# An attention and mixture-of-experts layer on one core: who issues the expert weights' loads, and where in the program

## The reference

```python
x = hidden_states                                   # 2 x 2048 x 512, float32
x = x + layernorm(attention(layernorm(x)))          # linear attention, 16 heads, 4 kv heads, D = 128
x = x + layernorm(moe(layernorm(x), wg, w1, v1, w2))

def moe(x):                                         # 4096 tokens, 32 experts, top 8, H = 512, F = 192
    scores = softmax(x @ wg.T)
    weights, idx = top_k(scores, 8); weights /= sum(weights)
    for each expert e, over the rows sent to it:
        h = silu(rows @ w1[e]) * (rows @ v1[e])
        out[token] += (h @ w2[e]) * weight
```

## Time and profile before

| | us |
|---|---|
| median of 3 runs | 2455.93 (2454.94 to 2457.64) |
| the profiled execution | 2444.98 |
| its span, first to last instruction | 2443.3 |
| TensorE busy in the span | 2227.0 (91%) |
| VectorE, ScalarE, GpSimd busy | 1486.4, 1233.1, 956.2 |

### The profile page before, as it was taken

One profiled execution on the slowest core, in us unless ns is written; L12 is line 12 of the kernel. 1 busy time (PEld: TensorE's weight loads), 2 busy tenths in 40 slices (PEclk: granted clock), 3 DMA queues, 4 the chain that ended last, 5 costly groups with the idle time before them and its releaser, 6 DMA issues.

```text
span 2443.3 us, 64606 instructions
## 1 busy us (share of the span) xinstructions
PE 2227.0 (91%) x11850; PEld 1919.5 (79%) x11851; DVE 1486.4 (61%) x4836; ACT 1233.1 (50%) x2643; POOL 956.2 (39%) x1128
## 2 busy tenths in 40 slices
PE   7999899999999999995699999989999899988980
PEld 5888588888868888884598888878889788978970
DVE  4455567777777777775555555565555655555546
ACT  3344456665656666663344454455444544444433
POOL 1222015555535555556233334333344333433432
PEclk9999899999999999997899999999999999999995
DMA  3233202333343233233898888877777877776767
GB/s 122 78 120 120 78 27 104 117 119 117 119 149 127 106 117 131 101 135 138 255 225 193 180 203 184 182 196 175 144 157 145 191 160 166 141 168 137 142 106 296
DMA packets 165230, 358.64 MB, mean 147 GB/s; under 512 B 21168, under 2 KB 21168, under 8 KB 165040
## 3 DMA queue, kind: packets, MB, share of 16 engines
q0 software_dynamic: 60512, 144.74, 28.5%
q1 hardware_dynamic: 91216, 173.89, 23.7%
q10 hardware_dynamic: 13440, 39.33, 4.9%
HBM read 178.21 MB, written 179.66 MB: 146 GB/s over the span
## 4 chain that ended last, share of the span: by engine, by line
PE 32%; DMA 7%; issue 6%; ACTq 2%; DVE 2%; POOL 2%; DVEq 1%; ACT 1%; POOLq 1%; SPq 0%
DMA moe_sum<-Y,aidx 6%; PE bank L469 6%; PE bank L471 5%; PE bank L470 5%; PE bank L460 4%; PE bank L486 2%; PE bank L479 2%; PE bank L490 2%; PE bank L488 2%; PE bank L487 2%; PE bank L489 2%; DMA LATE<-w_in 1%; POOL sorted_rows L1543 1%; ACTq L329 1%; ACT BIG L596 1%
## 5 line engine op out<-in xcount | busy, mean ns | idle before, releaser
L1477 POOL DMA_INDIRECT moe_sum<-Y,aidx x276 | 432.2, 1566 | 776.0 <-DMA moe_sum<-Y,aidx 416.7
L933 PE MATMUL bank<-WB,XH 128*128 128x512 f32 x1536 | 477.1, 392 | 0.0
L469 PE MATMUL bank<-WB,XL 128*128 x1104 | 398.2, 361 | 0.0
L471 PE MATMUL bank<-WB,XH 128*128 x1104 | 373.4, 338 | 0.0
L470 PE MATMUL bank<-WB,XH 128*128 x1104 | 371.5, 337 | 0.0
L933 PEld LDWEIGHTS bank<-WB,XH 128*128 128x128 f32 x1536 | 290.4, 189 | 58.3 <-issue 0.7
L933 PE MATMUL bank<-WB,XL 128*128 128x512 f32 x768 | 316.1, 412 | 10.3 <-DVE XL L1259 10.3
L933 PE MATMUL bank<-WB,SH 128*128 128x512 f32 x1024 | 318.1, 392 | 0.0
L713 DVE SCALAR_TENSOR_TENSOR BIG<-BIG,bank x276 | 95.9, 348 | 351.8 <-ACT BIG L531 274.1
L1543 POOL DMA_INDIRECT sorted_rows<-BIG,pos x256 | 265.6, 1038 | 94.6 <-issue 94.6
L531 ACT ACTIVATE BIG<-bank x276 | 91.3, 331 | 341.7 <-PE bank L471 319.9
(11 more groups left out here) (218 smaller groups left out, 4260.3 us busy)
## 6 DMA issues: line engine op xcount, KB each, us to landing
BIG<-sorted_rows SPq DMA_DIRECT2D x278, 274.0 KB
Y<-x_in SPq DMA_DIRECT2D x64, 256.0 KB, 2.8
RAW<-w_in ACTq DMA_DIRECT2D x15, 768.0 KB
LATE<-w_in ACTq DMA_DIRECT2D x15, 768.0 KB
sorted_rows<-BIG SPq DMA_DIRECT2D x33, 274.0 KB
moe_sum<-LATE SPq DMA_DIRECT2D x34, 256.0 KB, 3.0
LATE<-x_in SPq DMA_DIRECT2D x32, 256.0 KB
RAW<-wo_in SPq DMA_DIRECT2D x16, 512.0 KB, 3.7
```

The source lines that it names most:

```text
L469: nc.tensor.matmul(eu[s][:, 0:UP], XL[:, s, k, :], wh, start=k == 0, stop=False)
L471: last = nc.tensor.matmul(eu[s][:, 0:UP], XH[:, s, k, :], wl, start=False, stop=k == KC - 1)
L933: last = nc.tensor.matmul(ps, w, m, start=start and i == 0, stop=stop and i == len(terms) - 1)
L1477: nc.gpsimd.indirect_dma_start(acc_dram[:, :], bass.IndirectOffsetOnAxis(aidx[:, s:s + 1], 0), rows, None, compute_op=ALU.add).then_inc(s_ ...
```

## The change

SyncE's loop no longer goes by groups of four tiles but by expert. For expert e it waits for a fill of pads, issues the fill of expert e+8, waits on `s_elo` and issues the four loads of the weights of expert e+3; for 14 of the experts it then issues a load of `after_attention`; then it issues the row loads of tiles first+6 to first+n+5. Eight fills and the first six row loads stand ahead of the loop. The row ring keeps its four slots and the waits on `s_T` and `s_wr`. The four semaphores of the row loads become one, `s_ld`; SyncE waits before tiles g and g+1 (g even) until all loads before g have landed, and TensorE waits for the loads by pairs. ScalarE keeps the conversions and loses the wait on `s_elo` and the loads between the pieces. Six more entries of `at_tile` are set to zero, and four more row loads are issued at the end.

```diff
--- before.py
+++ after.py
@@ -38,6 +38,7 @@
 PIECES = [(k * UP, UP) for k in range(KC)] + [(W13, HID), (W13 + HID, HID)]
 FRING = 8
 XRING = 14
+AHEAD = 6
 FOUT = 4
 YSLOTS, RSLOTS = 4, 4
 
@@ -156,7 +157,7 @@
         rank = sb("rank", [P, EXPERTS])
         posf = sb("posf", [P, TOP_K])
         pos = sb("pos", [P, 2, TOP_K], u32)
-        AT, ES = MAX_TILES + 2, 4 * EXPERTS
+        AT, ES = MAX_TILES + 2 + AHEAD, 4 * EXPERTS
         tn = bq[:, 0:ES].rearrange("p (i n) -> p i n", i=4)
         step = bq[:, ES:ES + 2 * EXPERTS].rearrange("p (i n) -> p i n", i=2)
         table = bq[0:1, 2 * ES:2 * ES + 4 * EXPERTS].bitcast(i32).rearrange("p (i n) -> p i n", i=4)
@@ -242,11 +243,11 @@
 
         s_ewr, s_ehi, s_elo = [sem("ew_loaded0"), sem("ew_loaded1")], sem("ew_high"), sem("ew_low")
         s_pad0 = sem("padding_ready")
-        s_fill, s_fillx = [sem("pads_filled0"), sem("pads_filled1")], sem("spare_page_filled")
-        s_ld = [sem(f"rows_loaded{i}") for i in range(RSLOTS)]
+        s_fill, s_fill0, s_fillx = [sem("pads_filled0"), sem("pads_filled1")], sem("first_pads_filled"), sem("spare_page_filled")
+        s_ld = sem("rows_loaded")
         s_wr, s_T, s_exh, s_exl = sem("row_tails"), sem("e_transposed"), sem("e_high"), sem("e_low")
         s_U, s_sg, s_h = sem("e_up"), sem("e_silu"), sem("e_act")
         s_H, s_hh, s_hl = sem("e_act_transposed"), sem("e_act_high"), sem("e_act_low")
@@ -296,13 +297,16 @@
             return not isinstance(t, int) or 0 <= t - lag < TILES
 
 
+        def expert_word(eng, e):
+            word = eng.value_load(table[0:1, 0, bass.ds(e, 1)], min_val=512 + 32768, max_val=512 * 32768 - 1)
+            return word & 511, (word >> 9) & 63, word >> 15
         def each_expert(eng, convert, body):
 
             eng.wait_ge(s_tabd, 1)
 
             def one(e, q):
-                word = eng.value_load(table[0:1, 0, bass.ds(e, 1)], min_val=512 + 32768, max_val=512 * 32768 - 1)
-                first, n, before = word & 511, (word >> 9) & 63, word >> 15
+                first, n, before = expert_word(eng, e)
                 convert(e, q, before)
                 body(e, q, first, n)
                 return first + n
@@ -352,17 +356,19 @@
                 last.then_inc(s_elo, 1)
 
         def moe_sp(sp):
-            def fill_pads(e, i):
+            def fill_pads(e, done):
                 row = sp.value_load(table[0:1, 2, bass.ds(e, 1)], min_val=0, max_val=PAGES * PAGE)
-                sp.dma_start(sorted_dram[bass.ds(row, P), :], padrow[:, 0, :]).then_inc(s_fill[i], 16)
-            def load_rows(g, i):
+                sp.dma_start(sorted_dram[bass.ds(row, P), :], padrow[:, 0, :]).then_inc(done, 16)
+            def load_rows(g):
                 row = sp.value_load(at_tile[0:1, 2, bass.ds(g + 2, 1)], min_val=0, max_val=PAGES * PAGE)
                 sp.wait_ge(s_T, g + 1)
                 stand(sp)
                 sp.wait_ge(s_wr, g + 1)
                 stand(sp)
-                sp.dma_start(xr[:, i, :], sorted_dram[bass.ds(row, P), :]).then_inc(s_ld[i], 16)
+                wait(sp, s_ld, g // 2 * 32 if isinstance(g, int) else (g >> 1) * 32)
+                stand(sp)
+                sp.dma_start(BIG[:, at(XR, g & (RSLOTS - 1), ROW, ROW)], sorted_dram[bass.ds(row, P), :]).then_inc(s_ld, 16)
 
             def load_x2(f, r):
                 sp.dma_start(fx[:, bass.ds(r, 1), :, :].rearrange("p a j n -> p (a j) n"),
@@ -379,35 +385,51 @@
             sp.wait_ge(s_pad0, 5)
             sp.dma_start(sorted_dram[EXTRA * PAGE:EXTRA * PAGE + P, :], padrow[:, 1, :]).then_inc(s_fillx, 16)
             sp.wait_ge(s_tabd, 1)
-            for e in range(2):
-                fill_pads(e, e)
+            for e in range(AHEAD + 2):
+                fill_pads(e, s_fill0)
             for i in range(2):
                 sp.wait_ge(s_sc[i], TILES // 2 * TOP_K * 16)
             sp.wait_ge(s_fillx, 16)
+            sp.wait_ge(s_fill0, 16 * (AHEAD + 2))
             sp.wait_ge(s_tiles, 1)
-            def quad(p, fill=False):
-                for i in range(RSLOTS):
-                    g = RSLOTS * p + i
-                    if fill:
-                        sp.wait_ge(s_fill[i % 2], 32 * p + 16 * (i // 2) + 16)
-                        stand(sp)
-                    load_rows(g, i)
-                    if fill and (not isinstance(g, int) or g + 2 < EXPERTS):
-                        fill_pads(g + 2, i % 2)
-            FILLS = EXPERTS // RSLOTS
-            with sp.Fori(0, FILLS - 1) as p:
-                quad(p, True)
-            quad(FILLS - 1, True)
-            with sp.Fori(0, XRING) as f:
-                quad(f + FILLS)
-                load_x2(f, f)
-            quads = sp.value_load(pair_n[0:1, 0:1], min_val=TOKENS * TOP_K // P // 2, max_val=PAGES // 2) >> 1
-            with sp.Fori(FILLS + XRING, quads) as p:
-                quad(p)
+            for g in range(AHEAD):
+                load_rows(g)
             for i in range(2):
-                load_rows(RSLOTS * quads + i, i)
+                sp.sem_inc(s_fill[i], 16)
+            def body(e, q, first, n, x2=None):
+                i = q % 2
+                if not isinstance(e, int) or e + AHEAD < EXPERTS:
+                    sp.wait_ge(s_fill[i], (e - i) * 8 + 16)
+                    stand(sp)
+                if not isinstance(e, int) or e + AHEAD + 2 < EXPERTS:
+                    fill_pads(e + AHEAD + 2, s_fill[i])
+                if not isinstance(e, int) or e + 3 < EXPERTS:
+                    sp.wait_ge(s_elo, e + 2)
+                    stand(sp)
+                    load_weights(sp, e + 3, (q + 1) % 2)
+                if x2 is not None:
+                    load_x2(x2, x2)
+                with sp.Fori(0, n) as k:
+                    load_rows(nc.s_assert_within(first + k + AHEAD, AHEAD, MAX_TILES + AHEAD - 1))
+            with sp.Fori(0, 3) as r:
+                for q in range(WSETS):
+                    e = r * WSETS + q
+                    first, n, _ = expert_word(sp, e)
+                    body(e, q, first, n, e)
+            with sp.Fori(3, 6) as r:
+                for q in range(WSETS):
+                    e = r * WSETS + q
+                    first, n, _ = expert_word(sp, e)
+                    body(e, q, first, n)
+            for e in range(6 * WSETS, EXPERTS):
+                first, n, _ = expert_word(sp, e)
+                body(e, e % WSETS, first, n, e - 12 if e - 12 < XRING else None)
+                total = first + n
+            sp.wait_ge(s_ld, 16 * total + 16 * AHEAD)
+            stand(sp)
             pairs = sp.value_load(pair_n[0:1, 0:1], min_val=TOKENS * TOP_K // P // 2, max_val=PAGES // 2)
             for i in range(2):
                 sp.wait_ge(s_add[i], 16 * pairs + 16)
@@ -454,7 +476,7 @@
 
             def rows_t(g, i, p):
                 s = i % 2
-                pe.wait_ge(s_ld[i], 16 * p + 16)
+                pe.wait_ge(s_ld, 64 * p + (32 + 32 * (i // 2)))
                 pe.wait_ge(s_exl, g)
                 for k in range(KC):
                     last = nc.tensor.transpose(et[s][:, k * P:(k + 1) * P], xr[:, i, k * P:(k + 1) * P], ident[:, :])
@@ -494,7 +516,7 @@
                 word = pe.value_load(at_tile[0:1, 0, bass.ds(i, 1)], min_val=0, max_val=64 * EXPERTS - 1)
                 return (word & (WSETS - 1)) * WSET, ((word >> 6) & (WSETS - 1)) * WSET
 
-            pe.wait_ge(s_ld[0], 16)
+            pe.wait_ge(s_ld, 32)
             for k in range(KC):
                 last = nc.tensor.transpose(et[0][:, k * P:(k + 1) * P], xr[:, 0, k * P:(k + 1) * P], ident[:, :])
             last.then_inc(s_T, 1)
@@ -556,16 +578,10 @@
             def convert(e, q, before):
                 if isinstance(e, int) and e + 2 >= EXPERTS:
                     return
-                load = not (isinstance(e, int) and e + 3 >= EXPERTS)
                 act.wait_ge(s_D, before)
                 stand(act)
-                if load:
-                    act.wait_ge(s_elo, e + 2)
-                    stand(act)
                 for piece in range(len(PIECES)):
                     weights_high(act, e + 2, (q + 2) % WSETS, q % 2, piece)
-                    if load and piece < 4:
-                        load_weights(act, e + 3, (q + 1) % 2, piece)
 
             def body(e, q, first, n):
                 def tile(g):
@@ -674,6 +690,7 @@
             nc.vector.tensor_scalar(iota_g[:, :], iota_g[:, :], col[:, 2:3], None, ALU.is_ge).then_inc(s_cmp, 1)
             dve.wait_ge(s_tmm, 1)
             nc.vector.memset(at_tile[:, 1:3, 0:2], 0)
+            nc.vector.memset(at_tile[:, :, MAX_TILES + 2:AT], 0)
             nc.vector.tensor_copy(at_tile[:, 1, 2:2 + MAX_TILES], bank[7][0:1, 0:MAX_TILES])
             done(nc.vector.tensor_copy(iota_g[0:1, :], bank[6][0:1, 0:MAX_TILES]))
             settled()
```

## The result

| | median us | against before (95% interval) |
|---|---|---|
| before | 2455.43 (4 runs) | |
| changed | 2481.77 (4 runs, 2479.68 to 2484.84) | 1.0112 (1.0091 to 1.0133) |

That is +26.3 us, where +10.4 was forecast. The sign held. The measured time also lies inside the wide range (2445 to 2484), but only by 2 us and at the end that had been set for rival B; the forecast's own range (2460 to 2475) missed it, and the size is off by a factor of 2.5. The profiled executions took 2444.98 and 2483.32 us, 38 apart.

A forecast was written before the change was run, and what follows sets the result against it. TensorE, 91% busy, was taken as the bound; -14.5 + 22.4 + 2.5 = +10.4 us gave 2455.4 on the profiled execution, and 2466 with the median's 11 us difference. Own range 2460 to 2475, wide range 2445 to 2484.

The forecast's parts named there:

- rival B: Row loads queued behind weights and x2 starve TensorE: 0 to 3 us at six experts, 2481 us; chance 0.14.
- What bounds it: Expert stage: TensorE is busy 91%; only its idle time near expert changes, 62 us, can be gained.
- part 1: ScalarE converts without issuing loads: 20.5 us less TensorE idle time at expert changes, of which 14.5 us are kept.
- The slot behind the landing: ScalarE's conversion waits put down to L490, read as long done: 7.1 us in 2 places.
- Part 2: SyncE issues the weights, behind its row load: a cost of 18.4 + 1.5 + 2.5 = 22.4 us.
- the issue path: On SyncE the first weight DMA starts 3.0 us after the row issue, 1.8 us from e = 24 on.
- the price of the delay: Weights issued later land later at seven short-expert conversions: delays of 1.9 to 3.2 us, 18.4 us in sum.
- the places: Seven conversions that wait for weights, at 1317.6, 1623.1, 1908.0, 1917.4, 2021.4, 2155.8 and 2209.7 us, pay for the later issue.
- one more wait is new: SyncE's even row load waits for all earlier loads, delaying weights behind it at f = 167: +2.5 us (0 to 4).
- Part 3: Start of the experts: more fills ahead and TensorE waiting for a row pair cost +2.5 us (0 to 6).
- Rival A: Faster: the later weight issue costs nothing and the start is cheap, 2441 us, or 2450 with half; chance 0.22.
- C: No change: the weights' delay costs half as much and the start is free, 2452 to 2459 us; chance 0.19.

The follow-up runs named there:

- second profile: The kernel before and the changed kernel, each unchanged, profiled once more: 2454.91 and 2481.84 us.
- loads behind: Kernel before, with ScalarE issuing the four weight loads behind its six conversions instead of between them: 2438.96 us, 0.9951.
- weights back on ScalarE: Changed kernel with the weight loads back on ScalarE's queue, behind the six conversions: 2448.41 us, 0.9967.
- later, ScalarE's queue: Kernel with ScalarE's loads behind the conversions, the four loads moved into the expert's first tile, behind the evacuation: 2442.56 us, 0.9954.
- AHEAD = 4, SyncE's queue: Changed kernel with AHEAD = 4 for 6, so SyncE reaches the weight loads two tiles earlier: 2448.61 us, 0.9995.
- AHEAD = 5, SyncE's queue: Changed kernel with AHEAD = 5 for 6, so the weights are issued one tile earlier: 2455.94 us, 1.0003.
- fill behind, SyncE's queue: Changed kernel with SyncE's weight loads ahead of the fill of pads of the same expert: 2461.19 us, 1.0034.

## Why the prediction was right in sign and wrong in size

The mean moment at which the first weight DMA is issued, and at which the last lands, both counted from the end of the transposes of tile first+1 over the loads of experts 3 to 31, read from the timelines:

| kernel | issue | landing | ScalarE waits for weights | L479/L501 and L460/L482 idle | ratio |
|---|---|---|---|---|---|
| before (second profile) | 2.6 (2.8) | 11.5 (11.7) | 24.5 (30.5) | 53.9 (60.1) | 1 |
| loads behind | 3.0 | 11.7 | 29.1 | 48.5 | 0.9951 |
| weights back on ScalarE | 2.9 | 12.2 | 30.1 | 44.5 | 0.9967 |
| later, ScalarE's queue | 5.3 | 13.7 | 45.0 | 60.8 | 0.9954 |
| AHEAD = 4, SyncE's queue | 0.4 | 9.4 | 14.4 | 62.4 | 0.9995 |
| AHEAD = 5, SyncE's queue | 3.3 | 12.3 | 38.8 | 62.0 | 1.0003 |
| fill behind, SyncE's queue | 5.8 | 13.8 | 50.3 | 63.8 | 1.0034 |
| changed | 6.9 | 15.7 | 62.6 | 85.4 | 1.0112 |

The idle column is L479's (or its successor's) wait for the gate plus L460's for rows, in us of the profiled execution. From first issue to last landing the weights take 8.9 us before and 8.8 in the changed kernel: they are not slower in SyncE's queue, they are issued later.

- **What bounds it, and part 1 (right).** All 30 conversions took 2.80 to 2.81 us and all chains 3.27; the gate's distance fell from 10.05 to 3.95 us in sum. Together 18.1 of the forecast 20.5, and -12 us (-7 to -17) in the kernel that does only this, where 14.5 were to be kept.
- **The slot behind the landing (read wrongly).** The forecast said of the two waits put down to L490 that it "had long been done". It had not: the down product that frees the slot ended at 1917.06, with the weights landed at 1916.90, and at 2021.01, with the last landing on record at 2020.67. Each time the conversion started 0.35 us after the product. At the other five places the product ended 0 to 3.1 us ahead of the landing. So the kernel before had little to gain from earlier weights there, which the forecast did not see.
- **Part 2, the issue path (right).** 2.93 us from row issue to weight issue against 3.0 (3.2 in the mean of the 24 changes with a fill); SyncE's row issue waits for the tile that was named.
- **Part 2, the price of the delay (too high).** 18.4 us for 2.3 to 3 us at seven places. The run with the later loads had 16 us more of ScalarE's waits and 12 more of L479's, and at most some 7 us more time.
- **Part 2, the places (wrong).** Against the second profile of before, the changed kernel is 3.5 us late at tile 50, 29.6 at tile 145 and 28.5 at the end (its second profile: 3.0, 21.9 and 26.9). Of the seven priced places only one, the conversion of 1623.1, lies between tiles 50 and 145.
- **Part 2, "one more wait is new" (the step that failed).** It was priced at 2.5 us, at f = 167 alone; everywhere else the forecast left SyncE's row issue where it was before and added 3.0 us. But the row issue itself moved. Ahead of a change it came 4.0 us after the transposes in the mean, against 2.7 before and 3.1 with the weights back on ScalarE's queue. So the first weight issue came at 6.9 us in the mean and not at the 4.9 of the change at tile 29; 11 of 29 loads were issued later than 8 us. At 15 changes of 29 the row issue came over 2.6 us after the transposes (7 before, but 15 with the weights back too, by less). At six of the 15 the wait that ended just ahead of it was for a row landing (1.1 to 5.3 us): a row behind the weights holds SyncE, and SyncE brings the next weights late. At the others SyncE's own instructions fill part of the time: from the row issue of 1314.21 to the next one at 1322.67 it waits for nothing and spends 8.46 us on a fill, four weight issues, an x2 load and the table reads, while a tile takes 3.9 us.
- **What the runs show of it, and what not.** Taking the weights out of SyncE's program saves 35 us although all its other waits stay, and moving them forward within it saves 19. A mean issue 2.3 us later on ScalarE's queue costs under 8 us; the changed kernel's is 3.9 us later than there, which no run has on that queue. The changed kernel without its pair wait was not run either. So it is shown that the weights' place in SyncE's program costs the time. How much of it comes by the pair wait, and how much by the time that SyncE's own issues take, is argued from the trace.
- **TensorE's clock (left out of the forecast).** Between the first and the last transposes of rows the granted clock stood at the lower level (1.2 of 2.4 GHz) for 47.5 us before (64.0 in the second profile) and for 79.4 us in the changed kernel (85.9). TensorE's busy time (the stretch less its idle time), for the same matmuls, was 1118.4 (1123.0) and 1123.5 us (1128.6). In the means of the two profiles each, the 32.6 us between the kernels are 5.8 of a later first tile, 21.9 of idle time and 5.3 of longer busy time, less 0.4 behind the expert stage.
- **Part 3 (wrong as a term).** The first tile came 5 to 7 us later, where 2.5 was forecast: the fills were issued 1.7 us apart and not 1.2, and the last landed at 1186.0 and not at 1182. But making the first tile earlier gained nothing in the end.
- **Rival B (right in part).** L482 waited 17.4 us (10.7 in the second profile) for rows, at tiles 56, 60 and 84 in both. The forecast gave it 0.14 and held it for an alternative; it came together with the forecast's mechanism, since both hang on one queue. That the measured time is its 2481 is luck: its price was for starved rows alone. Rival A and C were not seen: the interval from issue to landing did not shrink.

The rule quoted under rival B (one queue is consumed in its order; Trainium skill, "DMA: Bandwidth & Descriptors", Queues, rings and completion order) fits this: at AHEAD = 6 the rows issued behind the weights made TensorE wait 17.4 us, with the weights on the other queue 1.5, and at AHEAD = 4, with the rows issued closer to their use, 36.5.

What stays open: how the loss divides between the pair wait and SyncE's own issues; and why the pair wait alone costs 10 us in the timed runs, of which 3 are seen at the start. The kernels "later" and "fill behind" are 19 us apart by their ratios but only 12.2 in their profiles; of these 3.8 lie at the first tile, 2.2 in TensorE's idle time and 5.2 in its busy time (58.2 and 66.2 us at the lower clock).

## What to carry to other kernels

When a load moves to another issuing engine, follow that engine's whole program for two rounds, not one: a wait on what was queued behind the load, and the time of the issues themselves, delay the next load too, so that a fixed delay can feed itself. Compare a round with the pace of the consumer (8.5 us against 3.9 here at an expert of one tile). If an engine issues and computes, try first whether issuing behind the computation is late at all. A wait that covers another (the slot behind the landing) caps what removing the first can give; look for it before pricing the gain.

## What the runs showed of the hardware

ScalarE's DMA issues behind six activations started 0.31 us after the first of them, with some 2.5 us of them still to run (their sum is 2.80 us): here an issue in program order behind a computation was not behind it in time. Between the pieces, the same four issues stretched the six activations from 2.80 us to 3.6 and up to 4.6 us.

1.3 MB of weights took 8.8 us from first issue to last landing on SyncE's queue, 8.0 there without the fill directly ahead, and 8.4 to 9.3 on ScalarE's in four kernels (means of 29 loads). A row load behind weights and x2 took 7.35 us instead of 2.94.

After TensorE's wait of 6.65 us the granted clock was 0.50 in 1329 to 1335 us, and four row transposes took 1.05 instead of 0.60 us.
